# The preparation of a recurrent scan on Trainium2: LayerNorm on ScalarE, the short convolution on TensorE, and a table of steps for all five queues

## The reference, cut to what matters

```python
xn = (x - mean) / sqrt(var + eps) * ln_gamma + ln_beta     # per token, 256 channels
left, right = split(xn @ W_up + b_up)                      # 128 channels each
u = silu(causal_conv3(left, conv_w) + conv_b)              # depthwise, 3 taps
delta = softplus(u @ W_delta + b_delta); B = u @ W_B; C = u @ W_C      # 64 states
h_t = exp(delta_t * A) * h_(t-1) + (delta_t * u_t) * B_t   # 128 channels x 64 states
y_t = sum over states of h_t * C_t + D * u_t
out = (y * silu(right)) @ W_down + b_down                  # and the residual is added
```

## Time and profile before

| | before |
|---|---|
| median of 3 runs | 5256.79 us (5256.36 to 5259.19) |
| the profiled execution, its own time | 5262.06 us |
| its span, first to last instruction | 5260.3 us |
| mean granted TensorE clock | 0.923 |
| busy share: TensorE, VectorE, ScalarE, GpSimd | 84%, 72%, 49%, 49% |
| chunk 0 of the scan ends (L1257 starts) | 2408.9 us |
| chunks 3, 5, 14, 15 end | 2924.2, 3437.9, 5051.1, 5161.7 us |

### The profile page before, as it was taken

One profiled execution on the slowest core, in us unless ns is written; L12 is line 12 of the kernel. 1 busy time (PEld: TensorE's weight loads), 2 busy tenths in 40 slices (PEclk: granted clock), 3 DMA queues, 4 the chain that ended last, 5 costly groups with the idle time before them and its releaser, 6 DMA issues. The chain is left out here.

```text
span 5260.3 us, 63028 instructions
## 1 busy us (share of the span) xinstructions
PE 4414.5 (84%) x22290; PEld 3249.8 (62%) x22290; DVE 3779.2 (72%) x5198; ACT 2552.0 (49%) x4722; POOL 2553.5 (49%) x1749
## 2 busy tenths in 40 slices
PE   6799999977999999589999657788888888888872
PEld 5688888866888888456666425455555555555530
DVE  5466666654666666378888999878878878888795
ACT  5544444455444444456566312355556565555542
POOL 2100000021000000366666528889889889989871
PEclk8899999988999999799999858999999999999996
DMA  2100000011000000234333312345444444544446
GB/s 70 39 17 21 21 22 21 23 35 39 17 22 21 21 24 21 77 115 133 131 125 129 100 42 76 106 131 155 128 133 149 142 127 144 147 135 140 119 158 275
DMA packets 241483, 467.31 MB, mean 89 GB/s; under 512 B 33936, under 2 KB 153104, under 8 KB 241168
## 3 DMA queue, kind: packets, MB, share of 16 engines
q1 hardware_dynamic: 216592, 429.72, 24.6%
q0 software_dynamic: 24576, 33.57, 3.7%
HBM read 393.87 MB, written 69.34 MB: 88 GB/s over the span
## 5 line engine op out<-in xcount | busy, mean ns | idle before, releaser
L1323 POOL TENSOR_TENSOR scan_drive_sb<-scan_b_wide_sb,scan_du_sb 128x1024 f32<-128x1024 f32 x512 | 1305.7, 2575 | 337.5 <-DVE scan_h_sb L1244 334.3
L1244 DVE TENSOR_TENSOR_SCAN scan_h_sb<-decay_bank,scan_state_sb,scan_drive_sb 128x512 f32<-128x512 f32 x896 | 1119.5, 1269 | 139.0 <-ACT decay_bank L1489 107.1
L1409 PE MATMUL y_bank<-scan_ch_sb,identity_sb 128*128 128x512 f32 x2048 | 1097.0, 632 | 0.8 <-DVE scan_temp_sb L1257 0.8
L1489 ACT ACTIVATE decay_bank<-scan_delta_sb,a_neg_sb 128x512 f32<-128x512 f32 x1024 | 701.8, 687 | 521.4 <-DVE scan_h_sb L1244 517.8
L824 PE MATMUL ybank<-v_low_hi_lo_sb,pt_hi_b_sb 128*128 128x384 f32 x2048 | 671.8, 361 | 20.4 <-DVE pt_lo_b_sb L714 15.8
L1251 DVE TENSOR_TENSOR scan_ch_sb<-c_pair,scan_h_sb 128x1024 f32<-128x1024 f32 x512 | 615.4, 1202 | 100.6 <-PE c_pair L1400 97.0
L767 POOL TENSOR_TENSOR acc_b_sb<-acc_b_sb,g_in_b_sb 128x256 f32<-128x256 f32 x64 | 47.4, 741 | 1274.8 <-DVE acc_b_sb L750 1274.8
L714 DVE TENSOR_TENSOR pt_lo_b_sb<-pt,pt_hi_b_sb 128x512 fp32r<-128x512 f32 x512 | 353.2, 690 | 411.6 <-ACT pt_hi_b_sb L867 411.6
L1400 PE MATMUL c_pair<-scan_cc_sb,select_state_sb 128*128 128x512 f32 x1024 | 385.2, 459 | 228.8 <-DVE scan_ch_sb L1251 228.0
L825 PE MATMUL ybank<-v_low_hi_lo_sb,pt_lo_b_sb 128*128 128x256 f32 x2048 | 573.3, 280 | 0.0
L858 ACT ACTIVATE p_b_sb<-scores,softmax_cols_b_sb 128x1024 f32<-128x1024 f32 x256 | 286.2, 1118 | 539.3 <-DVE softmax_cols_b_sb L708 400.2
(11 more groups left out here) (314 smaller groups left out, 10149.9 us busy)
## 6 DMA issues: line engine op xcount, KB each, us to landing
scan_b_wide_sb<-b_scratch SPq DMA_DIRECT2D x512, 512.0 KB
x_b_sb<-x SPq DMA_DIRECT2D x16, 512.0 KB, 4.8
g_scratch<-g_out_b_sb SPq DMA_DIRECT2D x16, 512.0 KB, 3.2
x_res_b_sb<-x SPq DMA_DIRECT2D x64, 128.0 KB, 2.2
g_in_b_sb<-g_scratch SPq DMA_DIRECT2D x64, 128.0 KB, 2.2
x_scratch<-x_res_b_sb SPq DMA_DIRECT2D x64, 128.0 KB, 1.7
xn_scratch<-xn_out_b_sb SPq DMA_DIRECT2D x64, 128.0 KB, 1.7
scan_xn_sb<-xn_scratch SPq DMA_DIRECT2D x16, 512.0 KB
```

The source lines that it names most:

```text
L1244: e.tensor_tensor_scan(k.h[i % H_BUFFERS][:, j, :], k.decay_banks[S % DECAY_BANKS][:, :], k.drive[i % DRIVE_BUFFERS][:, j, :], start, ALU. ...
L1323: e.tensor_tensor(k.drive[i % DRIVE_BUFFERS][:, :, :], k.b_wide[i % B_BUFFERS][:, :, :], k.du[c % 2][:, :].unsqueeze(1).broadcast_to([P, P ...
L1409: e.matmul(k.y_bank[:, :], consts.identity[:, :], k.ch[i % CH_BUFFERS][:, j, :], start=(n == 0), stop=(n == STATES - 1)).then_inc(k.s_y, 1)
L1489: e.activation(k.decay_banks[S % DECAY_BANKS][:, :], k.delta[c % 2][:, :], ACT.Exp, scale=wt.a[:, n:n + 1]).then_inc(k.s_decay, 1)
```

## The change

- Preparation and end of a chunk follow a table of steps (`STATISTICS_AT`, ..., `C_AT`; 38 steps) and `PAIRS_AT` (10 steps), the same for all queues; what reads a matmul's result stands a step after it.
- LayerNorm: GpSimd makes, besides rstd, -mean * rstd (`norm_shift_gpsimd`), and ScalarE applies both in place of VectorE (`apply`). gamma is multiplied into W_up, and beta goes through W_up into b_up, once ahead of the loop (`scan_weights_tensor`, `scan_weights_vector`).
- The transposed input: ScalarE writes the upper half straight from the bank, VectorE the lower half from the bank and the upper half; before, ScalarE made a copy and GpSimd both halves.
- The convolution: three fp32 matmuls by diagonal matrices (`taps`) into a fill of its own, "conv"; Silu reads it with conv_b as its bias. The two past columns are copied by ScalarE.
- The right half is first copied with its bias, and Silu is taken together with that of u.
- The upper halves of u and of the gated y move from GpSimd to ScalarE. -|z| becomes Abs on ScalarE and exp with scale -1.
- The lower half of C comes from the bank, without the copy.
- b_down is added by a matmul of one row of ones; GpSimd's addition goes, and SP's store waits for VectorE.

The diff, cut:

```diff
+STATISTICS_AT = (4, 5)
+APPLY_AT = (8, 9)
+TURNED_AT = (10, 11)
+LEFT_AT = 15
+RIGHT_AT = 17
+CONV_AT = 19
+DELTA_AT = 24
+DU_AT = 33
+B_AT = 33
+C_AT = 35
+PREPARE_STEPS = 38
+PAIRS_AT = (5, 7)
+DOWN_STEPS = 10
-PREPARE_STEPS = 1 + 4 + 2 + 2 + 1 + 1 + 1 + 1 + 4 + 3 + 1 + 1 + 1 + 3 + 1 + 2 * 4
...
+def norm_shift_gpsimd(e, w, k, n, call):
+    e.tensor_scalar(k.shift[:, 0, 0:n], k.moments[:, 0:n, 0], -1.0, None, ALU.mult).then_inc(k.s_shift, 1)
+    w.wait_ge(k.s_shift, 2 * call + 1)
+    w.wait_ge(k.s_rstd, call + 1)
+    e.tensor_tensor(k.shift[:, 1, 0:n], k.shift[:, 0, 0:n], k.rstd[:, 1, 0:n], ALU.mult).then_inc(k.s_shift, 1)
...
 def scan_vector(e, w, k, fills, wt):
-        norm_apply_vector(e, w, k.ln, tiles, tiles, c)
...
-            e.tensor_copy(k.left[:, 0:2], k.left[:, CHUNK:CHUNK + 2]).then_inc(k.s_head, 1)
...
-        e.tensor_scalar(C, k.left[:, 0:CHUNK], wt.conv_w[:, 0:1], wt.conv_b[:, 0:1], ALU.mult, ALU.add).then_inc(k.s_conv, 1)
-        for tap in (1, 2):
-            w.wait_ge(k.s_conv, 3 * c + tap)
-            e.scalar_tensor_tensor(C, k.left[:, tap:tap + CHUNK], wt.conv_w[:, tap:tap + 1], C, ALU.mult, ALU.add).then_inc(k.s_conv, 1)
...
-        e.scalar_tensor_tensor(A, X, -1.0, X, ALU.mult, ALU.min).then_inc(k.s_z, 1)
...
-        e.tensor_tensor(s[STATES:P, :], raw[STATES:P, :], f32(s[STATES:P, :]), ALU.subtract).then_inc(k.s_bc_lo, 1)
...
+    def turned_lower(c, ci):
+        w.wait_ge(k.s_yt_hi, DC * c + ci + 1)
...
+        e.tensor_tensor(k.yt_lo[:, ci, :], fills.bank("turned", c, ci), f32(k.yt_hi[:, ci, :]),
+                        ALU.subtract).then_inc(fills.emptied("turned", c, ci), 1)
...
+        e.tensor_tensor(s[STATES:P, :], fills.bank("bc", c, 1)[STATES:P, :], f32(s[STATES:P, :]),
+                        ALU.subtract).then_inc(fills.emptied("bc", c, 1), 1)
...
 def scan_gpsimd(e, w, k, fills, wt, consts):
-            e.tensor_scalar(k.yt_hi[:, ci, :], yt, 1.0, 0.0, ALU.mult, ALU.add).then_inc(k.s_yt_hi, 1)
-            w.wait_ge(k.s_yt_hi, 2 * c + ci + 1)
-            e.tensor_tensor(k.yt_lo[:, ci, :], yt, f32(k.yt_hi[:, ci, :]), ALU.subtract).then_inc(k.s_yt_lo, 1)
...
-        e.tensor_scalar(k.u_hi[:, :], k.u[c % 2][:, :], 1.0, 0.0, ALU.mult, ALU.add).then_inc(k.s_u_hi, 1)
...
-        e.tensor_scalar(k.u_hi[:, :], y, 1.0, 0.0, ALU.mult, ALU.add).then_inc(k.s_g_hi, 1)
...
-            e.tensor_tensor(out, out, wt.b_down[:, :].unsqueeze(1).broadcast_to([P, 2, D]), ALU.add).then_inc(k.s_bias, 1)
...
 def scan_tensor(e, w, k, fills, wt, consts):
+    def conv(c):
+        fills.wait_emptied(w, "left", c)
+        bank = fills.take(w, "conv", c)
+        for tap in range(3):
+            last = e.matmul(bank, wt.taps[:, tap, :], k.left[:, tap:tap + CHUNK], start=(tap == 0), stop=(tap == 2))
+        last.then_inc(fills.filled("conv", c), 1)
...
+            e.matmul(out, consts.ones[0:1, :], wt.b_down[:, :], start=True, stop=False)
...
 def scan_scalar(e, w, k, fills, wt):
+    def apply(c, half):
+        w.wait_ge(k.ln.s_shift, 2 * c + 2)
+        w.wait_ge(k.s_xn, 16 * (c + 1))
+        for j in range(2 * half, 2 * half + 2):
+            e.activation(k.xn[:, j, :], k.xn[:, j, :], ACT.Identity, bias=k.ln.shift[:, 1, j:j + 1],
+                         scale=k.ln.rstd[:, 1, j:j + 1]).then_inc(k.ln.s_normed, 1)
...
+        e.activation(k.yt_hi[:, ci, :], fills.bank("turned", c, ci), ACT.Copy).then_inc(k.s_yt_hi, 1)
...
+    def silus(c):
+        fills.wait_emptied(w, "gate", c)
+        e.activation(k.gate[c % 2][:, :], k.gate[c % 2][:, :], ACT.Silu).then_inc(k.s_gate, 1)
+        fills.wait_filled(w, "conv", c)
...
+        e.activation(k.u[c % 2][:, :], fills.bank("conv", c), ACT.Silu, bias=wt.conv_b[:, 0:1]).then_inc(fills.emptied("conv", c), 1)
...
+        e.activation(A, fills.bank("delta", c), ACT.Abs, bias=wt.b_delta[:, 0:1]).then_inc(k.s_z, 1)
...
-        e.activation(B[STATES:P, :], bank[STATES:P, :], ACT.Copy).then_inc(fills.emptied("bc", c, 1), 1)
...
+    def gated_upper(c):
+        w.wait_ge(k.s_gated, c + 1)
```

413 lines of the change are left out of this document (239 added, 174 removed).

## The result

The changed kernel takes 5181.84 us (median of 4 runs, 5176.68 to 5184.45), where the kernel before took 5256.57 beside it: the ratio is 0.9856, with an interval of 0.9839 to 0.9873, or 75 us less. The prediction was 5147. The profiled execution is the shortest of the four, 5176.68.

What follows compares the result with a forecast made beforehand. GpSimd was taken to bound beside the routed experts, VectorE the choice, TensorE fullest beside the shared experts. Terms -88, -14, -12, +5, -1 sum to -110: 5262.1 to 5152, or 5147 on the runs' scale; range 5045 to 5245.

Steps and rivals of the forecast that it cites:

- The stalls: Chunks 7 to 13: VectorE's SBUF-only instructions wait while GpSimd is busy, holding the recurrence; L1234 takes 4581 ns, L1977 678.
- GpSimd is the fullest, so its bounds count: I take 10: Beside the routed experts: GpSimd allows 7.6 to 11.9 us a chunk; 10 taken over 8.8 chunks, -88.
- The signs named for this case: GpSimd as limit, chance 0.58: chunks 7 to 13 near 172 us; busy VectorE 134, GpSimd 156, TensorE 159.
- TensorE, losing 5.3, follows as long as it has idle time: Beside the routed experts: convolution and b_down add 5.3 us a chunk to TensorE, costing nothing if its idle time covers it.
- rival D: Two shared banks: TensorE becomes the limit, 6.7 us a chunk exposed in 12.8 chunks, slower at 5333; chance 0.11.
- the gain of 3 a chunk: Beside the shared experts: taken between a gain of 7.4 and a loss of 5.3 us; four chunks, -12.
- VectorE's own saving counts in full: Choice of tokens, chunks 4 and 5: VectorE bounds at 93% busy, so its saved work shortens the stretch, -14 us.
- First preparation +5: Load to first drive: 38 steps for 35, half of +6 counted, and some 2 us for weights; between -5 and +12.
- End -1: End of the kernel: two additions of b_down (2.54 us) give way to short matmuls, -1 us.
- Rival C: ScalarE waits for GpSimd's shift and gated product, decays stand behind; 8 of 10 us go; 5225; chance 0.17.
- Rival B: VectorE's saving comes through in full, GpSimd's backlog being a product of the stalls; 199 us saved, 5058; chance 0.14.
- The rule weighed: Shared SBUF port: a one-instruction wait caps L1234 at 3.6 us; the trace's 7.47 was taken as a wait over several.

Runs made afterwards that it cites:

- The C part alone: Kernel before, with C's lower half taken from the PSUM bank, ScalarE's second copy gone and the subtraction two steps earlier: 5214.0 us, ratio 0.9910.
- experiment 12: Changed kernel with ScalarE copying C's lower half into SBUF again and VectorE subtracting there, in the same step: 5193.1 us, ratio 0.9870.
- experiments 3: Changed kernel with one more 128 x 512 product on GpSimd per chunk, into a tile nobody reads: 5186.2 us, ratio 0.9859.
- 4: Changed kernel with the lower halves of u and of the gated product made by VectorE instead of GpSimd: 5211.9 us, ratio 0.9910.
- experiment 6: Changed kernel with LayerNorm applied by VectorE again and GpSimd without the two shift steps: 5229.9 us, ratio 0.9941.
- 7: Changed kernel with the upper half of the gated product made by GpSimd again instead of ScalarE: 5191.1 us, ratio 0.9866.
- the one-pass form: Changed kernel with b_down added by two one-pass matmuls (rounded upper half and remainder) in place of each fp32 one: 5166.4 us, ratio 0.9825.

## Why the prediction was right or wrong

**Faster, and within the range: right.** 5182 lies in 5045 to 5245, 35 us above the forecast.

**The stalls: right.** "VectorE instructions that work in SBUF alone stand still while GpSimd is busy, and hold the recurrence behind them" carries most of the gain. The C part alone gave 47 us, LayerNorm 15 alone and 45 when undone, and putting two new instructions of that kind on VectorE cost 28 (with two new waits). VectorE's busy time came out as summed, 133.9 a chunk. That every such instruction stands still was too strong: experiment 12's took 0.7 us in SBUF alone where GpSimd had a gap.

**"GpSimd is the fullest, so its bounds count: I take 10": the step that failed.** One more product on GpSimd cost 0.35 us a chunk, and taking two instructions off it in favour of VectorE made the kernel slower. The size, 8.05 us a chunk against 10, was near by luck, for another reason. VectorE's work fell by 14.1 us a chunk, as summed (14.5); its idle time, of which 3.6 were to go, rose from 33.8 to 39.9 instead. The three waits for TensorE make 5.9 of that rise and the wait for GpSimd before L1271 makes 3.3, while "issue" before the recurrence fell by 3.0. The signs named for this case (172 us a chunk, VectorE 134, GpSimd 156, TensorE 159) were all met within 4 us, but they only restate the counts of the instructions; none of them says who waits for whom. The one that does, "issue" or GpSimd as VectorE's waits, came out half: "issue" nearly went. The 0.6 us for GpSimd's two shift instructions had no row; they took 0.45.

**"TensorE, losing 5.3, follows as long as it has idle time": the other one.** TensorE is idle 18.9 us in each of chunks 7 to 13, yet b_down costs 2.5 us a chunk there and a second set of the convolution 1.5. The sum had both at nothing there. b_down lies in a place where VectorE stands waiting: ahead of the down matmuls, behind a product of GpSimd, a copy of ScalarE and a subtraction of GpSimd. The prices were near together and not singly: 3.1 us a chunk of records for b_down against 2.1, 2.7 for the convolution against 3.2.

**Where the 35 us lie.** Between the two profiled executions the forecast missed by 25: 21 in chunks 6 to 14, 8 in chunks 1 to 3, 8 in chunks 4 and 5, 5 in chunk 15 and the end, less 11 that chunk 0 gave beyond its share and less 6 in layer 0, which the change doesn't touch. The other 10 come from the executions: the profiled one was above the median before and below it after. So chunk 0 hid about a quarter of what the other stages missed.

**Chunks 1 to 3: -0.6 for -9.** VectorE saved 19 us of work and waited as much more. TensorE is busy 94.6%, just below the 95 that was the sign of rival D, and the chunks stand at 171.6. TensorE's busy time rose by 15 us, and the rest of the stretch shrank by as much. The six profiles in which TensorE has the same instructions (the changed kernel, experiments 3, 4, 6, 7 and 12) agree: it is busy 484.8 to 491.8 us of 513.5 to 520.8, and the stretch is 28 to 31 us longer than that each time, 43 before. That is what a bound by TensorE looks like, which is D's mechanism, and the gain of 3 a chunk that the sum took was 0.2; D's price of a loss was not reached. The -4.4 without b_down and the +3.3 with the convolution twice point the same way but are no larger than that spread.

**Chunks 4 and 5: -6.2 for -14.** "VectorE's own saving counts in full" failed: its work fell by 20 us, more than the 14, and its idle time rose by 13. Leaving b_down out gives 4.1 us there and doubling the convolution costs 7.6, which would be TensorE again, but both lie within what the stretch varies by, so who takes the saving back stays open. The granted clock is 0.80 in this stretch, 0.96 in the others.

**Chunk 0: -14.4 where -3 was in the sum.** The two parts tried in the kernel before give 6.7 and 4.4 of it, and of the undone parts none takes it back. The granted clock of the chunk is 0.92 before, 0.95 and 0.93 with those two parts and 0.96 after, and the step table itself was in no experiment, so its share stays open, here and in the other chunks.

**First preparation +5: right,** 2.7 from load to first drive and 2.5 for the weights (15.3 us for 12.8). **End -1: wrong sign,** +2.6; without b_down it is 5.8 shorter and with b_down on GpSimd 4.3, so the "short matmuls" are what costs at the end.

**Rival C** had its mechanism (44.2 us of ScalarE's waits for the gated product) and not its price: undone, the waits turned up before the residual. **Rival B** fell as predicted, 5058 is far off.

**The rule weighed.** The prediction held the trace's 7.47 us against 3.6, the subtraction plus a wait of one drive. The Trainium skill, SBUF — State Buffer, "Who interferes with whom", says that whoever issues first has the shared port pair for its whole instruction and the other blocks. That the wait is over after one instruction was the prediction's reading; the section does not say who comes next. The rows of experiment 12 agree with the rule: no stall in a gap, held to the end of the drive when one runs (3553.45 + 2.88 is 0.56 us past the drive's end at 3555.77). The bound of one instruction doesn't hold: the 9.65 us in experiment 6 cover four GpSimd instructions, three of which started after VectorE's own, and VectorE's ended only when the last had ended.

## What to carry to other kernels

Price work moved to another engine by what lies between it and the next wait of the engine that runs the loop, not by that engine's idle share: 3.1 us in front of a wait cost 2.5 on an engine that was 11% idle, and 1.5 us that no wait of VectorE ends on cost 0.35 on one that was 10% idle. Follow the queues of the DMA too: b_down on GpSimd held up a store and, behind it, the load that VectorE needed next. Where GpSimd is busy, an instruction of VectorE that reads and writes SBUF alone is better given one PSUM input, or a step in which GpSimd is idle, or to ScalarE. And a busy share that comes out as forecast confirms the count of instructions, not the cause; add or take away one instruction per engine to see which one counts.

The faster kernel that the runs point to is the changed one with b_down on GpSimd as before the change (5163.8 us, 22 below it by the ratios); the one-pass form gives as much within the intervals (5166.4). The two were not joined with anything else.

## What the runs showed of the hardware

- A VectorE instruction of 128 x 256 in SBUF, 389 ns at its shortest, took up to 9.65 us beside a series of four GpSimd instructions (experiment 6); ScalarE does the same work in 583 to 602 ns each time.
- A VectorE subtraction of 64 x 512 in SBUF took 0.69 us beside an indirect DMA that GpSimd issued (3732.33 us beside 3732.16 in experiment 12), and 2.88 us beside a drive.
- A matmul of one row of contraction and 256 columns in the one-pass type took 300 to 415 ns in the mean by the records (the estimate was 110), as long as those of 128 rows beside it (305 to 421). The two that stand for one fp32 matmul come to 715 ns, the fp32 one to 768.
- Abs brought no table load: 39 before the decays in chunks 7 to 13, where there were 38.
